# Four kinds of turned rows by DMA transposes through DRAM in place of TensorE's turns, in an attention and expert block

## The reference

```python
xn = _layernorm(x)                                   # once, feeds both
# attention: a second layer norm with a gain, then
q = l2norm(xn2 @ Wq) * 4                             # (b, 8 heads, 2048, 64)
k, v = l2norm(xn2 @ Wk) * 4, xn2 @ Wv                # (b, 2048, 64), one head
attn = softmax(einsum('bhid,bjd->bhij', q, k))
s = layer_norm(einsum('bhij,bjd->bhid', attn, v) @ Wout) * out_norm_g
# experts: logits, top 2 of 8, capacity 2560 rows per expert
y = (gelu(xg @ w1 + b1) @ w2 + b2) * gate            # gathered rows, summed back
return x + s * silu(ffn)
```

## Time and profile before

| | |
|---|---|
| median of 3 runs | 2934.33 us (2927.1 to 2937.42) |
| the profiled execution, its own time | 2921.14 us |
| its span, first to last instruction | 2919.4 us |
| mean granted clock of TensorE | 0.975 |
| busy: TensorE, VectorE, ScalarE | 93%, 70%, 64% of the span |

### The profile page before, as it was taken

One profiled execution on the slowest core, in us unless ns is written; L12 is line 12 of the kernel. 1 busy time (PEld: TensorE's weight loads), 2 busy tenths in 40 slices (PEclk: granted clock), 3 DMA queues, 4 the chain that ended last, 5 costly groups with the idle time before them and its releaser, 6 DMA issues.

```text
span 2919.4 us, 138380 instructions
## 1 busy us (share of the span) xinstructions
PE 2718.4 (93%) x64261; PEld 1906.6 (65%) x64261; DVE 2049.7 (70%) x3077; ACT 1855.4 (64%) x2355; POOL 649.0 (22%) x428
## 2 busy tenths in 40 slices
PE   4999989998888898999999999999999999999996
PEld 3766666665555676666666666677666666666774
DVE  5888878898766785343344344338999999898986
ACT  6777767765555575555455555447777777776773
POOL 2111111112766610000000000002243343333311
PEclk8999999999989999999999999999999999999997
DMA  3222222101422202132223223111112121111101
GB/s 102 83 83 98 85 97 76 63 29 45 136 95 95 81 15 43 53 82 82 58 75 82 67 66 82 51 37 40 35 55 61 48 62 46 52 46 53 44 23 44
DMA packets 207857, 187.48 MB, mean 64 GB/s; under 512 B 99048, under 2 KB 185008, under 8 KB 207280
## 3 DMA queue, kind: packets, MB, share of 16 engines
q1 hardware_dynamic: 194992, 145.06, 16.7%
q0 software_dynamic: 12288, 33.57, 3.6%
HBM read 71.61 MB, written 85.98 MB: 54 GB/s over the span
## 4 chain that ended last, share of the span: by engine, by line
PE 81%; DVE 7%; issue 6%; ACT 5%; another core or an unknown queue 1%; DMA 0%; SPq 0%; POOL 0%; POOLq 0%; DVEq 0%; ACTq 0%
PE pair L597 20%; PE bank L625 16%; PE bank L665 13%; PE pair L651 13%; PE bank L636 9%; DVE arena L1162 3%; PE bank L538 3%; PE bank L580 3%; ACT arena L818 1%; PE bank L550 1%; PE bank L568 1%; ACT h_f L825 1%; PE bank L507 1%; PE bank L453 1%
## 5 line engine op out<-in xcount | busy, mean ns | idle before, releaser
L1162 DVE TENSOR_TENSOR arena<-arena 128x1024 bf16<-128x1024 f32 (+1 forms) x1032 | 1224.5, 1212 | 260.4 <-ACT arena L818 243.5
L818 ACT ACTIVATE arena<-pair 128x1024 f32<-128x1024 f32 (+1 forms) x1032 | 1043.5, 1018 | 388.5 <-PE pair L597 368.0
L625 PEld LDWEIGHTS bank<-vhl,arena 64*128 64x128 bf16 x32768 | 740.1, 95 | 335.4 <-issue 54.2
L625 PE MATMUL bank<-vhl,arena 64*128 64x65 bf16 (+1 forms) x32768 | 841.6, 191 | 66.4 <-issue 31.3
L597 PE MATMUL pair<-qT,kT 64*128 64x512 f16 x6144 | 866.9, 383 | 19.1 <-ACT arena L818 13.6
L636 PE MATMUL bank<-vhl,arena 64*128 64x65 bf16 x16384 | 616.8, 191 | 29.2 <-issue 25.1
L825 ACT ACTIVATE h_f<-pair,b1T 128x512 f32<-128x512 f32 x320 | 218.9, 684 | 383.2 <-PE pair L651 382.8
L1211 POOL TENSOR_TENSOR q_small<-q_small,minus_half 128x8 f32<-128x8 f32 x64 | 151.5, 2367 | 1360.8 <-DVE q_small L1075 1360.7
L636 PEld LDWEIGHTS bank<-vhl,arena 64*128 64x128 bf16 x16384 | 411.4, 95 | 38.3 <-issue 31.5
L665 PE MATMUL bank<-w_hl,arena 128*128 128x256 bf16 x3840 | 426.8, 273 | 0.4
L665 PEld LDWEIGHTS bank<-w_hl,arena 128*128 128x128 bf16 x3840 | 375.3, 98 | 53.4 <-DVE att L1178 2.1
(11 more groups left out here) (188 smaller groups left out, 1766.7 us busy)
## 6 DMA issues: line engine op xcount, KB each, us to landing
routed_rows<-h_f SPq DMA_DIRECT2D x80, 256.0 KB, 4.7
expert_rows<-att SPq DMA_DIRECT2D x40, 512.0 KB, 2.8
raw<-in_L_ffn_w SPq DMA_DIRECT2D x32, 512.0 KB
xn_rows<-s_hl SPq DMA_DIRECT2D x16, 512.0 KB, 3.1
xT_out<-xn_rows SPq DMA_DIRECT2D x64, 128.0 KB
w_lo<-in_L_attn_x SPq DMA_DIRECT2D x64, 128.0 KB
out<-w_lo SPq DMA_DIRECT2D x64, 128.0 KB
s_xin<-in_L_attn_x SPq DMA_DIRECT2D x12, 512.0 KB, 5.7
```

The source lines that it names most:

```text
L625: nc.tensor.matmul(bank[:, at:at + width], p_top[rows, s, cols, 1], V[rows, kb, of:of + width], start=(kb == 0 and qb == 0 and turn == 0 a ...
L818: nc.scalar.activation(p_f32[:, n % NP, columns(n)], pairs[n % 2][:, columns(n)], ACT.Exp).then_inc(exped, 1)
L1162: nc.vector.tensor_tensor(p_lo[:, n % NP, c], p_f32[:, n % NP, c], p_top[:, n % NP, c, 1], ALU.subtract).then_inc(lowed, 1)
```

## The change

All of xn, k, q and most of the output rows are now turned on the way through DRAM. The split rows are stored with a plain DMA (xn was stored already; `k_rows`, `q_rows` and `o_rows` are new), SyncE waits until the store has landed, and then issues DMA transposes of 512 rows by 128 columns, each of which fills one 128x512 piece of `xT`, `kT`, `qT` or `att` (which then holds `oT_group`, the turned output rows of the group). For a group these are four transposes for xn, four more when xn is fetched again for its keys (from the fourth group on; before, this was a plain store and load of the turned rows), two for k, eight for q and eight for o. The output rows of groups 7 and 15 (`BY_PE`) are still turned by TensorE. For the other 14 groups ScalarE also copies the high half of the output rows (`o_hi`), 56 copies of 128x512.

The slots move: the tiles of q are prepared two slots earlier, the turn of q stands at `Q_AT+12` of the last tile (58 slots after `base[g-1]`), the turn of o at slot 30 of the next group and the four projections at 35, 43, 51 and 59 (before 19, 35, 51 and 67), the router's logits at `S_AT+26` (before +18), and the combining of a late tile at 33, 45, 57 and 69 (before 17, 33, 49 and 65).

The core of the diff follows. `pe` is TensorE's list, `act` ScalarE's and `sp` SyncE's; the new functions on `sp` are the ones that issue the DMA transposes, and those for k and o have the same form as the ones shown.

```diff
-    xT_rows = nc.dram_tensor("xT_rows", [NG, P, 2 * DC, GP], F16).ap()
+    k_rows = nc.dram_tensor("k_rows", [T, 2 * P], F16).ap()
+    q_rows = nc.dram_tensor("q_rows", [T, H * P], F16).ap()
+    o_rows = nc.dram_tensor("o_rows", [T, 2 * INNER], BF16).ap()
...
     for t in range(GT, NT):
-        Q_AT.append(base[t // GT - 1] + 16 * (t % GT))
-    O_AT = []
+        Q_AT.append(max(base[0] + 1, base[t // GT - 1] + 16 * (t % GT) - 2))
...
+            O_SPLIT.append(base[g + 1] + 12 + 4 * j)
+            O_TURN.append(base[g + 1] + 30)
+            O_PROJECT.append(base[g + 1] + 35 + 8 * j)
+    C_AT = [base[XG + 1] + 20 + 13 * t if t < EARLY else O_SPLIT[t] + 8 if t // GT in BY_PE else
+            base[t // GT + 1] + 33 + 12 * (t % GT) for t in range(NT)]
...
             def prepare_q(t_id):
...
-                yield from clock.at(Q_AT[t_id] + Q_TURN)
-                bank, free = side.take(qT_copied, t_id + 1)
...
-                for h in range(H):
-                    t = nc.tensor.transpose(view[:, h * P:(h + 1) * P],
-                                            qhl[:, h // 2, h % 2, :, :].rearrange("p a b -> p (a b)"),
-                                            ident16[:, :])
...
                 for _, g, _, kb in halves(n):
-                    pe.wait_ge(qT_copied, GT * (g + 1))
-                    pe.wait_ge(kT_copied, BG * (g // BG) + kb // GT + 1)
+                    pe.wait_ge(qT_loaded, 16 * H * (g + 1))
+                    pe.wait_ge(kT_loaded, 16 * 2 * (BG * (g // BG) + kb // GT + 1))
...
-                yield from clock.at(Q_AT[t_id] + Q_TURN)
-                act.wait_ge(q_turned, t_id + 1)
-                act.wait_ge(scored, steps_to(g - 2) if g >= 2 else 0)
-                cast(qT[g % 2][:, :, j * P:(j + 1) * P], where["qT", t_id].bitcast(F16).rearrange(
-                    "p (h c) -> p h c", h=H)).then_inc(qT_copied, 1)
...
+                yield from clock.at(S_AT[g] + S_TURN[g])
+                sp.wait_ge(s_stored[g % 2], 16 * (g // 2 + 1))
+                if g > BG:
+                    sp.wait_ge(s_scored, g)
+                for k in range(2 * DC):
+                    nc.sync.dma_start(xT_of(g)[:, k, :], xn_turned[g, :, k * P:(k + 1) * P],
+                                      transpose=True).then_inc(x_turned, 16)
...
+            def prepare_q(t_id):
+                g, j = divmod(t_id, GT)
+                yield from clock.at(Q_AT[t_id] + 9)
+                sp.wait_ge(q_lo, t_id + 1)
+                nc.sync.dma_start(q_tiles[t_id], qhl[:, :, :, :, :].rearrange("p a k b n -> p (a k b n)")
+                                  ).then_inc(q_stored, 16)
+                if j == GT - 1:
+                    yield from clock.at(Q_AT[t_id] + 12)
+                    sp.wait_ge(q_stored, 16 * GT * (g + 1))
+                    if g >= 2:
+                        sp.wait_ge(scored, steps_to(g - 2))
+                    for k in range(H):
+                        nc.sync.dma_start(qT[g % 2][:, k, :], q_turned[g, :, k * P:(k + 1) * P],
+                                          transpose=True).then_inc(qT_loaded, 16)
```

## The result

The changed kernel took **3060.07 us** (median of 4 runs, 3044.45 to 3072.68) beside 2933.47 us for the kernel before: ratio 1.0431, 95% interval 1.0379 to 1.0483. It is slower; forecast were 2918 us (2860 to 2978) and a chance of 0.34 for slower, and the time lies outside the range. A second comparison, on another chip, gave 1.0459 (1.0412 to 1.0506).

The account below looks back on a forecast made before the run. TensorE was taken to bound early attention, with VectorE right behind late. Early -64 - 5 + 16.5 + 9 + 6 + 13 = -24 us, late +8, together -16: 2934.3 - 16 = 2918 us, range 2860 to 2978.

Parts of the forecast that it names:

- the output rows' stop: Ahead of each group's first output projection: about 1 us lacking, 2 late, 8 in group 2; 13 us early, 6 late.
- the queries' 14.9 us: From VectorE's low half to usable `qT`: 3.1 us for the store plus 11.8 us for eight transposes.
- the blocked queries: Five late boundaries: the queries' turn stands behind a combining waiting for VectorE; TensorE stops 6.6 us each, 33 us.
- 0.70 us per turn: Gain on TensorE per removed turn in attention: 0.56 us of queue plus 0.14 us of idle; 152 turns.
- Fully early, half late: Time taken off TensorE counts fully in early attention (64 us), half late (of 42 us), VectorE being a floor.
- The start: Ahead of the first scores nothing covers the DMA turns: scores at 83 us in place of 66.7, loss 16.5 us.
- 1.26 us per transpose: SyncE's queue: each DMA transpose keeps it 1.26 us (median) and lands 2.7 us from issue.
- the experts' wait: The experts' first matmul waited 5.6 us for its turned rows; earlier output projections were to gain 5 us.
- nothing lost for keys behind the start: Keys and xn for the router have 10 or more slots and are covered, so no waits were counted.
- The rule on the rate: DMA transposes as fast as regular DMAs, 350 to 400 GB/s: eight in about 3 us, stops zero except the start's.
- The turns come later and later: Rival, chance 0.25: SyncE's transposes take 2.9 us more to the last landing; about +50 us, 2984 us.
- VectorE becomes the bound early too: Rival, chance 0.10: of 64 us early only half counts, late nothing; +16 us or so, 2950 us.

Follow-up runs that it names:

- e2: Changed kernel with the output projections 7 slots later (42, 50, 58, 66): 2947.6 us, ratio 1.0444 to the kernel before.
- e7: Changed kernel with SyncE's second fetch of xn at slot 3 of a group in place of 24: 3043.0 us, ratio 1.0331 to the kernel before.
- e11: Changed kernel with queries and output rows brought back by one plain load in place of eight transposes, so not turned: 2924.5 us, ratio 0.9977.
- e8: Changed kernel with the queries' turn at slot 57 in place of 58, ahead of the combining's load: 3034.9 us, ratio 1.0321.
- e13: Kernel before with one of eight transposes and an eighth of the copy per turn of output rows and, from group 2, queries: 2892.3 us, ratio 0.9886.
- e9: e5 with the load of the next x rows issued 8 slots earlier: 2917.1 us, ratio 0.9914 to the kernel before.
- e3: Changed kernel with output projections 7 slots later, next group's queries prepared earlier, and xn's second fetch at slot 3: 2869.0 us, ratio 1.0165.
- e14: e6 with group 14's output projections at slots 38 to 59 and its combinings at 28 to 61: 2824.0 us, ratio 0.9965.
- e15: e9 with group 14's output projections at slots 38 to 59 and its combinings at 28 to 61: 2845.6 us, ratio 1.0047.
- e5: e3 with the start (xn and keys of the first four groups, queries of group 0) turned by TensorE: 2926.7 us, ratio 0.9994.
- e6: e9 with TensorE turning queries, keys and output rows through the early half, DMA transposes with slack behind the experts: 2906.3 us, ratio 0.9930.
- e12: e9 with plain loads in place of the transposes of queries and output rows, so not turned: 2917.6 us, ratio 0.9949.

## Why the prediction was wrong

- **Failed: the output rows' stop ("About 1 us is lacking per group").** Forecast were 19 us in all. Measured were 76 us of waits for `att`, and the gaps between steps 35 and 36 of 14 groups sum to 144 us for 44 before, 100 more. The step that failed is the need, which I put at the queries' 14.9 us; the cover of about 14 that this leaves was right (13.2 in group 10, 12.7 to 16.2 elsewhere). Needed were 19.8 us in group 10: 2.9 behind xn's second fetch, 4.1 from the store to the turn for 3.1, and 12.8 for the turn with a slow transpose, for 11.8. Over the groups it was 16.0 to 27.8. I named the fetch and its 5.2 us and yet counted 1 us per group. Shown by e2 (7 slots later: gone), e7 (the fetch) and e11 (the chain).
- **Mis-sized: the blocked queries.** 6.6 us each were forecast, 8.0 to 10.6 came, 9.7 of them at the end of group 10. The mechanism was right (e8). The turn took 12.6 us there for 11.9, and TensorE was done with the group at 2373.6, 3.4 us behind VectorE's `c_added`, not the 5.3 forecast from the earlier trace rows. Probably it came sooner because it has nothing to turn any more; no run shows this by itself. All gaps ahead of first scores grew by 73 us, for 55 forecast.
- **Mis-sized: 0.70 us per turn.** It was the occupied queue of the earlier trace rows and the wait for the bank; 0.32 came back for it (e13). "Fully early, half late" fell too: in e13's windows 32 turns early gave 10 to 13 us, 48 late 12 to 22, about alike. What holds e9's early groups at 121 to 126 us isn't settled: neither TensorE (433 of 496 us) nor VectorE (424) is full there.
- **The start**: 83 forecast, 86.7 measured; the last low half was 1.5 us later, and I left out the last keys' turn ahead of the queries' in the queue, 1.9 us.
- **Right**: 1.26 us per transpose with 2.6 us to landing, the experts' wait (its 5.6 us are gone, and the stage is 7.3 us shorter; 2.3 are left in the profile on chip B), nothing lost for keys behind the start; and the place of the longest stop for output rows, group 2, if not its length (14.1 for 8).
- **The rule on the rate** (Trainium skill, Advanced Engine Details and Errata, X-Bar Transpose (TRN2)): the trace doesn't agree. 1 MB in 11.2 us of issue is 93 GB/s, and the stops that it would have made zero are there.
- **The rivals.** "The turns come later and later" (2984 us) was nearest and still too low. It named longer landings; they stayed at 2.6 us, and what came later was the store and the turn's place in the queue. The sum of "VectorE becomes the bound early too" (2950) leaves out its own late half: with half of 8.3 us not gained in eight groups it is about 2983.

The profiled execution was to take 2905 us and took 3061. If every pause is taken at its length, output rows are 80 of these 156 us, queries 18, the start 4, and the experts give back 2. The other 56 are then the turns: against its stops the sum had counted 102 us of them, and the trace leaves 100 + 73 + 20 - 7 - 140 = 46. 152 turns at e13's 0.32 make 49. That the two agree so well is partly luck: late pauses cost some 2 us more than their length (e2 and e3), early ones less than half of it (e9), and these two don't have to cancel.

## What to carry over

Here a chain of eight DMA transposes took its issue time, 1.26 us each, and one landing. What such a chain needs must be read in us at its own place in the queue, from the last write to the last landing: counting slots hid 1 to 13 us of it. Its cover must be read after the change, since moved or removed work shifts it (3.4 us for 5.3 at the queries). Before a long chain is put into a queue that is issued in order, list what is behind it (here a load of x rows) and what is ahead (a load that waits for VectorE). Turns taken off an engine that is 92% busy gave back little over half of the time that they had occupied there (0.32 of 0.56 us), although ScalarE was relieved as well.

## What the hardware showed besides

Chips differ in kind. In the groups of the scatters e3, e14 and e15 took 241 to 254 us on chips A and E, and e5, e6, e9 and e12 took 296 to 307 on B, C and D. On those, TensorE shows waits for something that the trace names only as remote, in e6 and e9:

```profile
PE bank L675 <- remote: 27.8, 18, 2.9
```

```profile
PE bank L674 <- remote: 41.0, 24, 4.0
```

and none on A and E. These waits are shorter than the 50 us and more by which the stage differs, and most of them lie in it. What it is stays open, and so does how much of the changed kernel's loss is left on a quick chip, where it wasn't run. In 20 of the changed kernel's 30 turns of queries and output rows, one to three of the eight transposes take about 2.1 us for 1.26.
